# Gathered rows and W1 kept on chip without slots, with POOL waiting for the landing of table t-2

## The reference

```python
emb = jax.vmap(lambda tab, idx: tab[idx])(tables, cat_features)      # 26 x 512 x 128
emb_btd = jnp.transpose(emb, (1, 0, 2))
wide_num = jax.nn.relu(numerical @ w_wide + b_wide)                  # 512 x 1
linear_output = jnp.sum(emb_btd, axis=1) + wide_num                  # 512 x 128
x = jnp.concatenate([numerical, emb_btd.reshape(512, 26 * 128)], axis=1)
x = jax.nn.relu(x @ W1 + b1)                                         # 512 x 256
x = jax.nn.relu(x @ W2 + b2)                                         # 512 x 128
return jax.nn.sigmoid(x @ W3 + b3 + linear_output)                   # W3: 128 x 1
```

## Time and profile before

| | |
|---|---|
| median of 3 runs | 145.59 us (145.54 to 146.35) |
| span of the profiled execution | 144.4 us, first to last instruction |
| median less that span | 1.2 us: what lies around the instructions, and the difference between executions |
| POOL busy | 99.5 us, 104 gathers of 0.95 us among it |
| PE busy | 88.3 us |
| DVE, ACT busy | 28.6, 20.4 us |
| DMA | 10.74 MB, 74 GB/s on average |

### The profile page before, as it was taken

One profiled execution on the slowest core, in us unless ns is written; L12 is line 12 of the kernel. 1 busy time (PEld: TensorE's weight loads), 2 busy tenths in 40 slices (PEclk: granted clock), 3 DMA queues, 4 the chain that ended last, 5 costly groups with the idle time before them and its releaser, 6 DMA issues.

```text
span 144.4 us, 1243 instructions
## 1 busy us (share of the span) xinstructions
PE 88.3 (61%) x278; PEld 46.0 (32%) x278; DVE 28.6 (20%) x75; ACT 20.4 (14%) x42; POOL 99.5 (69%) x111
## 2 busy tenths in 40 slices
PE   0768197609751792666734917906936609988881
PEld 0307142205320440231303404404502205545771
DVE  2302012202220201221211302202012202113451
ACT  0401011101110110110201101101101101122342
POOL 2577777777777777777777777776777776777400
PEclk9999999995999569977996895995599985699999
DMA  4413443462336446646345282582372571242311
GB/s 102 125 55 45 51 55 90 86 91 55 91 82 87 51 67 99 68 80 102 85 62 89 47 116 55 60 106 70 43 99 76 76 106 51 82 85 55 50 45 36
DMA packets 8756, 10.74 MB, mean 74 GB/s; under 512 B 2874, under 2 KB 7091, under 8 KB 8755
## 3 DMA queue, kind: packets, MB, share of 16 engines
q0 software_dynamic: 3328, 6.82, 33.9%
q1 hardware_dynamic: 4421, 3.73, 8.9%
q10 hardware_dynamic: 1006, 0.17, 0.7%
HBM read 10.45 MB, written 0.26 MB: 74 GB/s over the span
## 4 chain that ended last, share of the span: by engine, by line
DMA 35%; POOL 27%; PE 16%; issue 12%; POOLq 1%; DVE 0%; ACT 0%
DMA emb<-in_L_rec_tables,staged 32%; POOL emb L196 23%; PE turn L237 8%; PE first_layer L244 6%; POOL emb_tail L196 4%; DMA emb_tail<-in_L_rec_tables,row_idx 2%; DMA emb<-in_L_rec_tables,row_idx 2%; POOLq L54 1%; PE first_layer L295 1%; PE mlp L307 1%; PE scalars L317 0%; POOLq L206 0%; ACT y L487 0%; DVE h L421 0%; PE turn L285 0%
## 5 line engine op out<-in xcount | busy, mean ns | idle before, releaser
L196 POOL DMA_INDIRECT emb<-in_L_rec_tables,staged x88 | 83.2, 946 | 27.8 <-issue 23.5
L244 PE MATMUL first_layer<-emb_t,w 128*128 128x512 f32 x96 | 57.3, 731 | 0.3 <-ACT emb_t L466 0.3
L237 PE MATMUL turn<-ident,emb 128*128 128x128 f32 x96 | 20.3, 349 | 46.5 <-DMA emb<-in_L_rec_tables,staged 41.4
L237 PEld LDWEIGHTS turn<-ident,emb 128*128 128x128 f32 x96 | 14.0, 176 | 68.3 <-DMA emb<-in_L_rec_tables,staged 59.0
L466 ACT COPY emb_t<-turn 128x512 f32<-128x512 f32 x24 | 14.1, 586 | 109.0 <-PE turn L237 109.0
L244 PEld LDWEIGHTS first_layer<-emb_t,w 128*128 128x128 f32 x96 | 21.0, 241 | 17.0 <-issue 16.3
L381 DVE TENSOR_TENSOR emb_sum<-turn,emb_sum 128x512 f32<-128x512 f32 x23 | 15.9, 692 | 38.0 <-ACT emb_t L466 38.0
L369 DVE COPY staged<-row_idx 128x4 int32 (+1 forms) x22 | 4.4, 206 | 57.4 <-DMA emb<-in_L_rec_tables,staged 57.4
L196 POOL DMA_INDIRECT emb<-in_L_rec_tables,row_idx x8 | 7.7, 965 | 5.1 <-DVE row_idx L359 2.9
L196 POOL DMA_INDIRECT emb_tail<-in_L_rec_tables,row_idx x8 | 7.6, 946 | 2.4 <-issue 2.4
L295 PE MATMUL first_layer<-emb_tail_t,w_tail 128*128 128x128 f32 x32 | 4.9, 282 | 0.0
(11 more groups left out here) (33 smaller groups left out, 21.4 us busy)
## 6 DMA issues: line engine op xcount, KB each, us to landing
w<-in_L_rec_W SPq DMA_DIRECT2D x24, 128.0 KB, 2.6
emb<-in_L_rec_tables,staged POOLq DMA_INDIRECT x88, 3.6
w_tail<-in_L_rec_W SPq DMA_DIRECT2D x1, 256.0 KB, 2.9
out<-y SPq DMA_DIRECT2D x4, 64.0 KB, 1.5
w<-in_L_rec_W ACTq DMA_DIRECT2D x1, 128.0 KB
emb<-in_L_rec_tables,row_idx POOLq DMA_INDIRECT x8, 3.7
emb_tail<-in_L_rec_tables,row_idx POOLq DMA_INDIRECT x8, 3.1
cat_sb<-in_r_cat_features SPq DMA_DIRECT2D x1, 52.0 KB
```

Source lines behind the costliest of these rows:

```text
L196: nc.gpsimd.indirect_dma_start(tile, None, rows, bass.IndirectOffsetOnAxis(ap=index, axis=0)).then_inc(landed, 16)
L237: mm = nc.tensor.transpose(turn[par][:, chunk(c)], emb[:, par, c, :], ident[:, :])
L244: mm = nc.tensor.matmul(first_layer[k][:, :], w1[:, par, chunk(k)], emb_t[:, par, :], start=False, stop=False, skip_group_check=True)
```

## The change

- `emb` holds all 26 tables and `w1` all of W1; `staged` and its copies on DVE are gone, and so are the loops on all engines.
- POOL waits ahead of table t (from t = 3 on) for the landing of table t-2, and for nothing that PE does. Ahead of the two late tables (24 and 25) it waits for the landing of table 22, and after half of them for that of table 23.
- W1 comes through SP at the start in four DMAs of 2, 6, 9 and 9 tables, behind nothing.
- The 128 row numbers of the first gather have their own path: SP loads them first (one 4-byte word to a partition), three DVE steps make them. The full set is loaded by ACT's queue. DVE takes the steps of both in turn.
- `emb_t` has four slots in place of two.
- In the last part DVE doesn't add tiles to `emb_sum`. PE does it: `add_tile` multiplies the identity by the gathered tile into a PSUM bank `final`, `add_body` adds `emb_sum` in the same way, and the third layer goes into the same bank with W3 copied to 128 columns. ACT's sigmoid reads that bank, with the wide term as its bias; DVE's add of the wide term is gone.
- PE's order in the last part is a new one.
- The product by `w_wide` and the turning of the small vectors come ahead of the first table on PE.

In the diff, removed lines of the functions printed above are mostly left out.

```diff
-        emb = sb("emb", [P, PAIR, CH, D])
-        emb_t = sb("emb_t", [P, PAIR, B])
-        emb_tail = sb("emb_tail", [P, CH, PAIR, D])
-        emb_tail_t = sb("emb_tail_t", [P, CH, PAIR, P])
+        emb = sb("emb", [P, T, CH, D])
+        emb_t = sb("emb_t", [P, SLOTS, B])
+        late_t = sb("late_t", [P, TILES, P])
...
+            with nc.allow_non_contiguous_dma(reason="one index for each partition"):
+                sp.dma_start(first_cat[:, :], cat[0:1, 0:P].rearrange("a p -> p a")).then_inc(first_loaded, 16)
+            for i, loaded in enumerate(w1_loaded):
+                lo, hi = W1_CUTS[i], W1_CUTS[i + 1]
+                sp.dma_start(w1[:, lo:hi, :], W1[NUM + lo * D:NUM + hi * D, :].rearrange("(t d) n -> d t n", d=D)
+                             ).then_inc(loaded, 16)
...
+            def gather(t, c, index, landed):
+                nc.gpsimd.indirect_dma_start(emb[:, t, c, :], None, rows, bass.IndirectOffsetOnAxis(ap=index, axis=0)
                                              ).then_inc(landed, 16)
...
+            def column(t, c):
+                return row_idx[:, t * CH + c:t * CH + c + 1]
+            gp.wait_ge(first_steps, 3)
+            gather(0, 0, first_row[:, :], gathered[0])
+            gp.wait_ge(rows_ready, 1)
+            for t in range(BODY):
+                if t > AHEAD:
+                    gp.wait_ge(gathered[t - AHEAD], WHOLE)
                 for c in range(CH):
...
-                    gp.wait_ge(staged_ready[par], step)
-                    gp.wait_ge(turned[par], step)
...
+                    if t + c > 0:
+                        gather(t, c, column(t, c), gathered[t])
+            gp.wait_ge(gathered[BODY - AHEAD], WHOLE)
+            for c in range(CH):
+                if c == CH // 2:
+                    gp.wait_ge(gathered[BODY - AHEAD + 1], WHOLE)
+                for g in range(LATE):
+                    gather(BODY + g, c, column(BODY + g, c), late_gathered[c * LATE + g])
...
+            def turn_table(t):
+                pe.wait_ge(gathered[t], WHOLE)
+                if t >= 2:
+                    pe.wait_ge(added, t - 1)
                 for c in range(CH):
...
+                    mm = nc.tensor.transpose(turn[t % 2][:, chunk(c)], emb[:, t, c, :], ident[:, :])
+                mm.then_inc(turned, 1)
+            def sum_table(t):
+                if t in W1_CUTS:
+                    pe.wait_ge(w1_loaded[W1_CUTS.index(t)], 16)
+                pe.wait_ge(copied, t + 1)
+                for k in range(KH):
+                    mm = nc.tensor.matmul(first_layer[k][:, :], w1[:, t, chunk(k)], emb_t[:, t % SLOTS, :],
+                                          start=False, stop=False, skip_group_check=True)
+                mm.then_inc(used, 1)
+            turn_table(0)
+            for t in range(1, BODY):
+                turn_table(t)
+                sum_table(t - 1)
...
+            def turn_tile(n):
+                c, g = divmod(n, LATE)
+                pe.wait_ge(late_gathered[n], 16)
+                if n < 2:
+                    pe.wait_ge(added, BODY - 1 + n)
+                    pe.wait_ge(late_copied, n - 1)
+                nc.tensor.transpose(turn[n % 2][:, 0:P], emb[:, BODY + g, c, :], ident[:, :]
+                                    ).then_inc(late_turned, 1)
+            def add_tile(n):
+                c, g = divmod(n, LATE)
+                nc.tensor.matmul(final[c % 2][:, 0:D], ident[:, :], emb[:, BODY + g, c, :],
+                                 start=False, stop=False, skip_group_check=True)
+            def sum_tile(n):
+                c, g = divmod(n, LATE)
+                pe.wait_ge(late_copied, n + 1)
...
-            def turn_sum_and_layer2(c):
...
+            def add_body(c):
+                if c == 0:
+                    pe.wait_ge(added, BODY)
+                    pe.wait_ge(wide_ready, 1)
+                    pe.wait_ge(vecs_ready, 1)
                 if c >= 2:
                     pe.wait_ge(y_ready, c - 1)
-                nc.tensor.transpose(mlp[c % 2][:, P:2 * P], emb_sum[:, chunk(c)], ident[:, :])
+                nc.tensor.matmul(final[c % 2][:, 0:D], emb_sum[:, chunk(c)], ident[:, :],
+                                 start=True, stop=False, skip_group_check=True)
+            def layer2(c):
                 for k, ready in enumerate([h1_low_ready, h1_high_ready]):
...
             def layer3(c):
                 pe.wait_ge(h2_ready, c + 1)
...
+                    pe.wait_ge(w3_ready, 1)
+                nc.tensor.matmul(final[c % 2][:, 0:D], h2[:, chunk(c)], w3_wide[:, :],
+                                 start=False, stop=True, skip_group_check=True).then_inc(final_done, 1)
+            turn_tile(0)
+            sum_table(BODY - 1)
+            for c in range(CH):
+                n = c * LATE
                 if c >= 1:
-                    turn_tile(c, 0)
-                    sum_tile(c - 1, 1)
-                turn_tile(c, 1)
...
-                    layer3(c - 2)
-                sum_tile(c, 0)
...
-                    sum_tile(c, 1)
+                    turn_tile(n)
+                    layer2(c - 1)
+                add_body(c)
+                add_tile(n)
+                sum_tile(n)
+                turn_tile(n + 1)
                 if c >= 1:
-                    turn_sum_and_layer2(c - 1)
...
+                    layer3(c - 1)
+                add_tile(n + 1)
+                sum_tile(n + 1)
+            layer2(CH - 1)
...
+            dve.wait_ge(first_loaded, 16)
+            nc.vector.tensor_scalar(first_lim[:, :], first_cat[:, :], float(-V), float(V - 1), ALU.max, ALU.min
+                                    ).then_inc(first_steps, 1)
             dve.wait_ge(cat_loaded, 16)
...
+            nc.vector.tensor_scalar(cat_lim[:, :], cat_sb[:, :], float(-V), float(V - 1), ALU.max, ALU.min
+                                    ).then_inc(cat_steps, 1)
+            dve.wait_ge(first_steps, 1)
+            nc.vector.tensor_scalar(first_neg[:, :], first_lim[:, :], 0.0, float(V), ALU.is_lt, ALU.mult
+                                    ).then_inc(first_steps, 1)
+            dve.wait_ge(cat_steps, 1)
+            nc.vector.tensor_scalar(cat_neg[:, :], cat_lim[:, :], 0.0, float(V), ALU.is_lt, ALU.mult
+                                    ).then_inc(cat_steps, 1)
+            dve.wait_ge(first_steps, 2)
+            nc.vector.tensor_tensor(first_row[:, :], first_neg[:, :], first_lim[:, :], ALU.add
+                                    ).then_inc(first_steps, 1)
+            dve.wait_ge(cat_steps, 2)
+            nc.vector.tensor_tensor(cat_row[:, :], cat_neg[:, :], cat_lim[:, :], ALU.add).then_inc(cat_steps, 1)
             dve.wait_ge(base_ready, 1)
             dve.wait_ge(index_turned, 1)
...
+            nc.vector.tensor_tensor(row_idx[:, :], idx_bank[:, 0:T * CH], base[:, :, :].rearrange("p t c -> p (t c)"),
...
-                    relu_h2(c - 2)
...
-                    relu_h1_high(c - 1)
-                add_tile(c, 0)
...
-                    add_wide(c - 2)
-                add_tile(c, 1)
...
+            for c in range(CH):
+                relu_h1_high(c)
+                relu_h2(c)
...
+            for t in range(BODY):
+                act.wait_ge(turned, t + 1)
+                if t >= SLOTS:
+                    act.wait_ge(used, t - SLOTS + 1)
+                nc.scalar.copy(emb_t[:, t % SLOTS, :], turn[t % 2][:, :]).then_inc(copied, 1)
+            def copy_tile(n):
+                act.wait_ge(late_turned, n + 1)
+                nc.scalar.copy(late_t[:, n, :], turn[n % 2][:, 0:P]).then_inc(late_copied, 1)
...
             def squash(c):
...
-                nc.scalar.activation(y[:, c, :], mlp[c % 2][:, P:2 * P], ACT.Sigmoid,
...
+                act.wait_ge(final_done, c + 1)
+                nc.scalar.activation(y[:, c, :], final[c % 2][:, 0:D], ACT.Sigmoid,
+                                     bias=wide[:, c:c + 1]).then_inc(y_ready, 1)
+            act.wait_ge(vecs_ready, 1)
+            act.wait_ge(wide_ready, 1)
+            for c in range(CH):
+                copy_tile(c * LATE)
+                copy_tile(c * LATE + 1)
+                relu_h1_low(c)
                 if c >= 1:
...
+                    squash(c - 1)
             squash(CH - 1)
```

279 lines of the change are left out of this document (66 added, 213 removed).

## The result

The changed kernel takes 146.74 us (median of 15 executions, 146.52 to 148.43); the kernel before takes 145.6 (15 executions, 145.11 to 146.5). The ratio is 1.0103 [1.0079, 1.0128]; it takes in all executions, and 4 of the 15 lie 1.7 us above the others, so the two medians alone give 1.0078. Forecast were 146.2, the range 143.9 to 148.2, and "within 1%" as the likeliest case, up to 147.05; the time lies near the upper edge of that case. The profiled execution took 146.84 us with a span of 145.0, which is the span forecast.

A forecast was written before the change was run, and what follows sets the result against it. POOL's gathers were taken to bound the kernel, PE the new tail. First gather -0.7, stalls -1.0, late tile 7 +2.7, shorter end -0.5: +0.5 to +0.6, span 145.0; with 1.2 above it, 146.2 us, range 143.9 to 148.2.

The forecast's parts named there:

- within 1%: Whole kernel: the likeliest case, the forecast's own sum, 145.4 to 147.0 us; "same" had a chance of 0.58.
- Part 1: Start: the first gather waits for a small index load only, starting at 3.95, a gain of 0.7 us.
- Part 2: POOL's waits: both stalls go, 1.0 us gained, with the other steps staying at 1.25 us a gather.
- Part 3: W1 loaded at the start: cost 0, up to 1 us if a landing there passes 6.25 us.
- third rival: POOL's waits: landings pass 6.25 us and POOL stands 0.3 to 0.5 us each, 148 to 151; chance 0.05.
- Part 4: Tail on PE: rounds of 2.93 us against 2.5 of feed; tile 7 2.7 us late, 0.5 gained behind it.
- The sum: Whole kernel: all terms together give +0.5 to +0.6 us, span 145.0 against 144.4.
- The 1.2 of the forecast: Whole kernel: the median 145.59 taken as 1.2 us above the span, left as it is.
- +0.6: Whole kernel: upper end of the net change, +0.5 to +0.6 us.
- the 1.0 of stalls: POOL: two longer stands, ahead of the gathers at 100.56 and 120.88, 0.69 + 0.31 us, both to go.
- landing-bound tail: Tail: rival in which tile 7 is turned when it lands, 143.4, or 144.8 with half of it; chance 0.17.
- Lower clock in the tail: Tail: rival in which PE's lower clock reaches the sums or rounds, 147.4 to 148.7 us; chance 0.2.

The follow-up runs named there:

- e7b: Changed kernel with its first gather put back behind the whole index block; 147.79 us, ratio 1.0167 to the kernel before.
- e4: Changed kernel without any of POOL's waits for landings, each gathered row in its own place; 146.69 us, ratio 1.0121 to the kernel before.
- e8b: Changed kernel with POOL waiting, from table 2 on, for PE's turning of table t-2 in the body; 148.55 us, ratio 1.0235 to the kernel before.
- e5b: Changed kernel with W1 for tables 2 to 23 loaded one by one behind PE's use; 146.88 us, ratio 1.0086 to the kernel before.
- e1: Changed kernel with the last part's steps reordered on PE, ACT and DVE, same PE passes; 144.85 us, ratio 0.9976 to the kernel before.
- e2: Changed kernel in its own order without `add_body` and `add_tile`, output lacking the sum over tables; 144.95 us, ratio 1.0003 to the kernel before.
- e3: e1's order, with DVE in place of PE adding the late rows to `emb_sum`; 144.59 us, ratio 0.9925 to the kernel before.
- e9b: e3 with table 25 ahead of 24 in each late chunk, on the usual chip; 144.26 us, ratio 0.9921 to the kernel before.
- e9: e3 with table 25 ahead of 24 in each late chunk, on the chip where the kernel before takes 174.15 us; 199.15 us.

## Why the prediction was right, step by step

- **Part 1, first gather at 3.95:** 3.92. The index landed just ahead of 2.88, not at 2.7, but DVE started each step a little before the one ahead was through, so that all took 0.75 us and not 1.0. Gain 0.74 against 0.7; e7b prices undoing it at 1.05, since the changed kernel's whole block is ready 0.4 later than before (first gather at 5.07 against 4.66 in the earlier trace rows).
- **Part 2, POOL:** no gap over 0.30, last gather at 132.87 (132.9). Both stalls are gone, and e4 puts the new waits at nothing. But the stalls were those of one execution: in e8b, with the same wait for PE, they did not come.
- **Part 3, W1 for nothing:** the price holds (e5b: ratios 1.0086 and 1.0103, intervals overlapping), its reason does not. I had read the Trainium skill ("DMA: Bandwidth & Descriptors", section Queues, rings and completion order) as one W1 packet of wait for a gather's. The first gather's first packet started 5.35 us after its issue, and gathers 0 to 7 landed after 7.03, 7.01, 6.54, 6.16, 6.05, 5.70, 5.61 and 5.26 us. Three of them are past the 6.25 of the third rival. They cost nothing, because 6.25 us is what the last gather of a table has, and these are the first three of table 0, which POOL never waits for. Its first wait asks for table 1, whose last gather landed at 18.09, 1.0 us ahead of table 3's first gather (19.08); in the traces of e1 to e4 the same margin is 0.6 to 1.2 us. The forecast had 1.27 to spare, beside the longest landing of the kernel before (4.98): it had the delay behind the burst too small, and the margin was enough all the same. W1's last part landed at 16.6, not by 16.
- **Part 4, the tail:** tile 1 turned at 130.39 (130.4), odd tiles 3.02 us apart (2.93), tile 7 turned at 139.43 (139.2). That is 3.3 us after its landing (2.7): 0.2 of the difference comes from the rounds, the rest from a landing at 136.15 in place of 136.4. Sigmoid 3.26 behind (3.15). e1 and e2 show that the round is the cause.
- **The sum:** span 145.0 as forecast, but two errors cancel in it, and that was luck. The last sigmoid began at 142.69, 0.4 later than forecast (144.0 less 1.7). From there to the end it is 2.3 us, and not the 2.6 of the kernel before, which the forecast took over as the store's time. There it was partly POOL's: its DRAIN ended 18.1 us after 126.0, at 144.1, and SP, behind the last store, was through at 143.9.

```profile
L54 POOLq DRAIN  x1: 18145/18145/18145, 126.0 to 126.0; - x1
...
L54 SPq DRAIN  x1: 7/7/7, 143.9 to 143.9; - x1
```

  In the changed kernel POOL's is through at 142.4 and SP at 144.8, so the end follows the store alone. The 0.5 us by which the median is off come from the base: in every profiled execution of this study the time is 1.8 to 1.95 above its span, also in that of the kernel before (146.35, span 144.4), which was thus 0.75 above its kernel's median of 145.6. The 1.2 of the forecast is that median less the span of a longer execution. I added +0.6 to the median, though the 1.0 of stalls may not be in a median execution. Had I taken the forecast span plus the profiled execution's own 1.95, 146.95 would have come out, 0.2 from 146.74.
- **The rivals:** landing-bound tail: excluded in this order, and real in another (in e1 tile 7 is turned 0.4 us after its landing). Lower clock in the tail, forecast 147.4 to 148.7 at a chance of 0.2: it is what e4's profiled execution shows, at 148.26, and 4 of the changed kernel's 15 executions have such a time. It was no either-or but a share of executions, and the median is one of the others.

## What to carry to other kernels

When a producer is made faster, work out the consumer's round: what stands in series between two of its pick-ups, against the feed. Here 3.02 against 2.5 us turned 1.76 us won into 0.9 lost at the last sigmoid, and the order of a few steps on PE was worth 1.9 us (e1), with DVE's adds 0.9925 [0.9902, 0.9947] of the kernel before (e3). Before stalls seen in one profile are booked as gain, set that execution's own time against the median: 0.75 of this one's 1.0 us may have been in no median execution. A load made early is free only by the margin of the first wait behind it: measure that margin, here 1.0 us. And ask what else the program's end waits for: in none of the 14 traces did it come sooner than 9.7 us after the start of POOL's last gather (e9b), so e3 had only 0.2 to 0.3 us left to win.

## What the runs showed of the hardware that I had not expected

- A burst of 3.4 MB of W1 on SP's queue held the first packets of an indirect gather back by 5.35 us; landing 7.0 us against 2.8 without it (e5b). Without it the first packet started 1.9 us after the issue, so the burst put it off by 3.4 us. The same page of the Trainium skill says that an engine drains a whole packet, typically 9 to 17 descriptors and at most 64, from one ring before it switches. An estimate from the page's 64 and this case's profile (4112 pieces of 0.9 KB each on SP's queue, 332 GB/s over 16 engines) is 2.8 us for one such packet of W1, and 0.4 to 0.7 for 9 to 17. So the delay is nearer to one full packet than to the one small piece that I had in mind; which it was, no run here shows.
- It also held back ACT's loads of the small vectors and W2: PE's first `final` work (L202) waited for them until 12.5 us, where in e5b it began at 9.7 without a wait, and table 0 was turned at 14.4 (11.4 in e5b). Nothing of it reached the end, as e5b's time shows.
- POOL's closing DRAIN ended 9.5 us after the start of its last gather in every trace, and the program's last instructions come behind it: it ended e9b, and the kernel before by 0.26 us.
- On one chip, where the kernel before took 174 us, ACT began its copies in e9 up to some 17 us after PE's transposes were through while POOL was issuing gathers; after that PE and ACT went on at 2.15 us a table.
